# A two-layer attention and expert kernel: the last delay chain of the tail as one block, steps of the attention's set-up and routing moved, the ternary product's ends divided

## The reference, cut to what matters

```
x = x + attention(layernorm(x), ctx)          # 16 heads of 8, causal mask
x = x + experts(layernorm(x))                 # 64 experts, top 8, sigmoid gates normalised by their sum + 1e-8, plus a shared one
x = x + delay_attention(layernorm(x), ctx)    # circular correlation of Q and K by FFT, mean over the channels of a head,
                                              # the 4 best delays, softmax over them, V rolled and summed, then Wo, bo
x = x + ternary(x)                            # layernorm with gamma, beta; weight / (mean|weight| + 1e-5) rounded to -1, 0, 1;
                                              # xn clipped at max|xn| * (128 - 1e-5) / 128; product scaled by mean|weight|
```

## Time and profile before

| | |
|---|---|
| timed runs | 1245.01, 1246.98, 1247.70 us; median 1246.98 |
| the profiled execution's own time | 1246.12 us |
| its span | 1244.3 us (1.8 us lie around it) |
| PE / PE weight load busy | 97% / 80% of the span |
| DVE / ACT / POOL busy | 85% / 74% / 62% |
| mean granted TensorE clock | 0.992 of full |
| attention ends, experts run, tail runs, ternary runs | about 285, to 1090, to 1221, to 1244 us |

### The profile page before, as it was taken

How to read it: one execution, slowest core, us unless ns; L and a number is a source line. 1 busy time by engine, 2 the same in 40 slices (tenths; PEclk the granted TensorE clock), 3 DMA queues, 4 the chain that set the end, 5 groups by cost and what they waited for, 6 DMA issues and landing times. The chain is left out here.

```text
span 1244.3 us, 28539 instructions
## 1 busy us (share of the span) xinstructions
PE 1211.1 (97%) x9899; PEld 993.6 (80%) x9899; DVE 1061.3 (85%) x2053; ACT 922.2 (74%) x1601; POOL 768.6 (62%) x845
## 2 busy tenths in 40 slices
PE   8999999999999999999999999999999999899986
PEld 6878787777888888888888888888888887799975
DVE  6999998997797897987987987978979877699986
ACT  5899998877777777777777677777777776777761
POOL 4667677855576565665665755765656624477773
PEclk8999999999999999999999999999999999999998
DMA  6411111108867767777677687677676775111004
GB/s 147 105 32 34 32 32 32 35 13 196 185 171 180 176 177 173 175 184 175 163 184 182 161 191 183 172 179 178 177 174 174 184 185 142 43 31 31 19 2 135
DMA packets 126174, 159.99 MB, mean 129 GB/s; under 512 B 20840, under 2 KB 59504, under 8 KB 126064
## 3 DMA queue, kind: packets, MB, share of 16 engines
q1 hardware_dynamic: 120976, 156.16, 50.7%
q10 hardware_dynamic: 5088, 2.43, 0.7%
HBM read 152.25 MB, written 6.29 MB: 127 GB/s over the span
## 5 line engine op out<-in xcount | busy, mean ns | idle before, releaser
L1081 POOL TENSOR_TENSOR e_ml<-e_m,e_mh 128x1024 fp32r<-128x1024 f32 x80 | 192.5, 2407 | 145.0 <-ACT e_mh L1234 143.6
L1234 ACT CAST e_mh<-e_m 128x1024 fp32r<-128x1024 f32 x256 | 267.2, 1044 | 6.4 <-DVE e_m L1161 6.4
L1224 ACT ACTIVATE shared<-shared 128x1024 f32<-128x1024 f32 x171 | 172.7, 1010 | 133.0 <-PE shared L1260 131.5
L1166 DVE TENSOR_TENSOR e_ml<-e_m,e_mh 128x1024 fp32r<-128x1024 f32 x176 | 241.7, 1373 | 25.7 <-ACT e_mh L1234 25.7
L1161 DVE TENSOR_TENSOR e_m<-shared,raw 128x1024 f32<-128x1024 f32 x171 | 207.1, 1211 | 61.2 <-ACT shared L1224 61.2
L1270 PE MATMUL e_py<-e_mh,wdl 128*128 128x512 f32 x528 | 209.3, 396 | 0.0
L1269 PE MATMUL e_py<-e_mh,wdh 128*128 128x512 f32 x528 | 208.0, 394 | 0.0
L1273 PE MATMUL e_py<-e_ml,wdh 128*128 128x512 f32 x528 | 167.4, 396 | 0.1
L1258 PE MATMUL shared<-r_xh,wuh 128*128 128x512 f32 x349 | 141.4, 405 | 0.1
L1260 PE MATMUL shared<-r_xl,wuh 128*128 128x512 f32 x349 | 137.9, 395 | 0.0
L1259 PE MATMUL shared<-r_xh,wul 128*128 128x512 f32 x349 | 137.8, 395 | 0.0
(11 more groups left out here) (243 smaller groups left out, 2811.8 us busy)
## 6 DMA issues: line engine op xcount, KB each, us to landing
raw<-gates_scratch SPq DMA_DIRECT2D x512, 256.0 KB, 4.2
x_res<-in_x_dram SPq DMA_DIRECT2D x64, 64.0 KB, 1.8
xcT<-in_ctxT_dram SPq DMA_DIRECT2D x64, 64.0 KB, 1.9
held<-in_ctx_dram SPq DMA_DIRECT2D x32, 128.0 KB, 2.1
raw<-in_L_ffn_W_up_dram SPq DMA_DIRECT2D x4, 512.0 KB, 4.7
raw<-in_L_ffn_W_down_dram SPq DMA_DIRECT2D x4, 512.0 KB, 5.7
gates_scratch<-raw SPq DMA_DIRECT2D x16, 128.0 KB, 2.3
out_dram<-t_res SPq DMA_DIRECT2D x8, 256.0 KB, 2.6
```

Source lines behind the costliest of these rows:

```text
L1081: nc.gpsimd.tensor_tensor(flat(ml[k][:]), flat(m[k][:]), flat(mh[k][:]).bitcast(F32), ALU.subtract).then_inc(m_low[1], 1)
L1166: nc.vector.tensor_tensor(flat(ml[k][:]), flat(m[k][:]), flat(mh[k][:]).bitcast(F32), ALU.subtract).then_inc(m_low[0], 1)
L1224: nc.scalar.activation(flat(pu[k]), flat(pu[k]), ACT.Silu).then_inc(silued, 1)
L1234: nc.scalar.copy(flat(mh[k][:]), flat(m[k][:])).then_inc(m_high, 1)
```

## The change

Attention: the output bias (`p_bias`) is multiplied ahead of step 5 on PE, without the wait for `w_chain` 2, and copied out ahead of step 5's `row_max` on DVE; `weight_mean` takes the place behind it; `p_beta` goes to a free column of the score buffer and into step 5's `scores`. The first chunk's roots stand behind the keys (`expand`) in step 12. The routing weights are made in steps 61 and 62, ahead of the variance operations, and what follows them is one step later.

Tail: group 7's `l_sums` ends in step 34, its chain is correlated in the middle of step 35 behind five extra matmuls, and its eight DVE operations run without a break behind the residual add of step 35 (`CHAIN_STEP`); the turn and transform follow in step 36. From then on POOL's root and offset stand one step later. Extra matmuls that nobody reads (`stay_busy`) are put into the last steps (the entry for `STEPS - 1` falls on a step where `l_pt` no longer runs) and behind them.

Ternary: two and three extra matmuls around the one for the maximum; DVE clips chunk 0 in two parts (128 and 384 columns); the last chunk is added and stored in two halves, one from ACT, one from SP.

```diff
-        p_beta = pob[:, 400:401]
+        p_beta = shared[:, 0, 4 * S:4 * S + 1]
...
-                late = {4: weight_sums, 5: weight_mean, 6: weight_inverse, 7: weight_round, 8: weight_upper, 9: weight_lower}
+                late = {4: weight_sums, 5: output_bias, 6: weight_inverse, 7: weight_round, 8: weight_upper, 9: weight_lower}
...
                     if isinstance(t, int) and t == 5:
-                        dve.wait_ge(o_bias_made, 1)
-                        nc.vector.tensor_copy(braw[:, 2:4, :], p_bias.unsqueeze(1).to_broadcast([3, 2, D])).then_inc(o_bias_out, 1)
+                        weight_mean()
...
                         expand(t - 3, (r - 3) % 2)
+                    if isinstance(t, int) and t == 12:
+                        norms.roots(pool, cst["mhalf"], 0, idle["pool"])
...
+                    if isinstance(t, int) and t == looped + 13:
+                        routing.weigh_all(pool, nc.gpsimd, "pool", 0)
+                    if isinstance(t, int) and t == looped + 14:
+                        routing.weigh_top(pool, nc.gpsimd, "pool", 0)
                     if live(t, 0, n_tiles):
...
-                    if isinstance(t, int) and t == 12:
-                        norms.roots(pool, cst["mhalf"], 0, idle["pool"])
-                    if isinstance(t, int) and t == looped + 13:
-                        routing.weights(pool, nc.gpsimd, "pool", 0)
-                    if isinstance(t, int) and t == looped + 15:
+                    if isinstance(t, int) and t == looped + 16:
                         routing.gates_of(pool, nc.gpsimd, "pool", 0)
...
@@ in scores @@
+                    if isinstance(t, int) and t == 2:
+                        pe.wait_ge(w_chain, 1)
+                        nc.tensor.matmul(p_beta, cst["ones"][:], wabs[:], start=True, stop=True).then_inc(w_summed, 1)
...
                         pe.wait_ge(w_out, 1)
+                        nc.tensor.matmul(p_bias, bv1col[:].to_broadcast([P, 3]), cst["w1T"][:, 3, :], start=True, stop=False)
+                        nc.tensor.matmul(p_bias, cst["ones"][0:1, 0:3], bo1row[:], start=False, stop=True).then_inc(o_bias_made, 1)
...
+    LAST_GROUP = N // 4 - 1
+    CHAIN_STEP = N + 3
...
@@ POOL, tail @@
-                    if on(s, 11):
-                        n = s - 11
+                    lag = 11 if s < CHAIN_STEP else 12
+                    if on(s, lag) and s != CHAIN_STEP:
+                        n = s - lag
...
@@ DVE, tail, behind the add of step 35 @@
+                    if s == CHAIN_STEP:
+                        top_of(LAST_GROUP)
+                        shift(LAST_GROUP)
+                        mark(LAST_GROUP)
+                        choose(LAST_GROUP)
+                        keep(LAST_GROUP)
+                        add_up(LAST_GROUP)
+                        invert_sum(LAST_GROUP)
+                        scale(LAST_GROUP)
...
+                    if on(s, 4) and s != CHAIN_STEP:
+                        sum_up(s - 4)
+                    if s == CHAIN_STEP - 1:
+                        sum_up(N - 1)
...
@@ PE, tail @@
+                def stay_busy(count):
+                    for _ in range(count):
+                        nc.tensor.matmul(pf[0][:, 0, 0, :], cst["ident"][:], cst["ident"][:], start=True, stop=True)
...
+                    if s == CHAIN_STEP:
+                        stay_busy(5)
+                        correlate(LAST_GROUP)
...
+                    if s == CHAIN_STEP + 1:
+                        turn_weights(LAST_GROUP)
...
+                    if s == CHAIN_STEP + 1:
+                        transform_weights(LAST_GROUP)
...
+                        stay_busy({STEPS - 3: 2, STEPS - 2: 4, STEPS - 1: 6}.get(s, 0))
...
+                stay_busy(4)
...
@@ DVE, ternary @@
-                clip(0)
+                for some in (slice(0, P), slice(P, 512)):
+                    nc.vector.tensor_scalar(columns(0)[:, some], columns(0)[:, some], bound[:, 0:1], bound[:, 1:2], ALU.min, ALU.max).then_inc(clipped_dve, 1)
                 clip(1)
...
+                for half in range(2):
+                    dve.wait_ge(multiplied, CHUNKS + half)
+                    add_rows(CHUNKS - 1, 2 * half, 2 * half + 2, (py[3][:, 0:2, :], pg_half)[half])
...
@@ PE, ternary @@
+                stay_busy(2)
                 pe.wait_ge(chain, 2)
                 nc.tensor.matmul(pg[:, 0:P], cst["ones"][:], diag[:], start=True, stop=True).then_inc(across, 1)
+                stay_busy(3)
...
-                sp.wait_ge(stored, 16 * CHUNKS)
+                store_half(sp, 1)
+                sp.wait_ge(stored, 16 * (CHUNKS + 1))
```

More of the change, by code:

```diff
@@ L1710, in _ @@
                     if g is not None:
[L1711 to L1715 removed]
+                        transform_weights(g)
                     if on(s, 2):
@@ L1725, in _ @@
                     k = group(s, 7)
-                    if k is not None:
-                        pe.wait_ge(summed, 4 * (k + 1))
-                        at_least(pe, c_out, k)
-                        at_least(pe, chosen, k)
-                        if k == 0:
-                            pe.wait_ge(preset, 1)
-                        for i in range(2):
-                            ins = nc.tensor.matmul(ext[:, :, 0:S], sums[:, k % 2, i, :], cst["idft_corr"][:, i * P:i * P + P],
-                                                   start=(i == 0), stop=(i == 1))
-                        ins.then_inc(correlated, 1)
+                    if k is not None and k != LAST_GROUP:
+                        correlate(k)
+                stay_busy(4)
 def ternary(nc, cst, x_res, xnT, amax, out, sem):
@@ L1780, in clip, with add_rows @@
                     nc.vector.tensor_scalar(columns(c), columns(c), bound[:, 0:1], bound[:, 1:2], ALU.min, ALU.max).then_inc(clipped_dve, 1)
-                clip(0)
+                for some in (slice(0, P), slice(P, 512)):
+                    nc.vector.tensor_scalar(columns(0)[:, some], columns(0)[:, some], bound[:, 0:1], bound[:, 1:2],
+                                            ALU.min, ALU.max).then_inc(clipped_dve, 1)
                 clip(1)
-                for c in range(CHUNKS):
+                def add_rows(c, first, last, product):
+                    nc.vector.scalar_tensor_tensor(res[:, c, first:last].rearrange("p j d -> p (j d)"),
+                                                   product.rearrange("p j d -> p (j d)"), cst["beta"][:],
+                                                   x_res[:, 4 * c + first:4 * c + last, :].rearrange("p j d -> p (j d)"),
+                                                   ALU.mult, ALU.add).then_inc(summed, 1)
+                for c in range(CHUNKS - 1):
                     if c + 3 in BY_DVE:
@@ L1800, in _, with stay_busy @@
             def _(pe):
+                def stay_busy(count):
+                    for _ in range(count):
+                        nc.tensor.matmul(py[3][:, 0, :], cst["ident"][:], cst["ident"][:], start=True, stop=True)
+                stay_busy(2)
                 pe.wait_ge(chain, 2)
                 nc.tensor.matmul(pg[:, 0:P], cst["ones"][:], diag[:], start=True, stop=True).then_inc(across, 1)
+                stay_busy(3)
                 for c in range(CHUNKS):
                     by_dve = sum(b <= c for b in BY_DVE)
-                    if c in BY_DVE:
-                        pe.wait_ge(clipped_dve, by_dve)
-                    else:
+                    if c in BY_DVE and c > 0:
+                        pe.wait_ge(clipped_dve, by_dve + 1)
+                    if c not in BY_DVE:
                         pe.wait_ge(clipped_pool, c + 1 - by_dve)
```

102 lines of the change are left out of this document (68 added, 34 removed).

## The result

The changed kernel's median is 1237.97 us (five runs, 1236.96 to 1241.75) against 1246.90 for the kernel before beside it; the ratio is 0.9935, interval 0.9918 to 0.9953. The forecast was 1238.7, from 1235.8 to 1243. The profiled execution of after took 1237.64 us with a span of 1235.8: 8.48 us less than that of before, where the sum had 7.45.

The account below looks back on a forecast made before the run. PE, busy 97% of the span at 0.992 of full clock, was taken as the bound. Attention 3.3, chain 2.3, extra matmuls 0.55 and ternary 1.3 gave 7.45 us off 1246.12: 1238.7 us, range 1235.8 to 1243.

Parts of the forecast that it names:

- Output bias: Attention step 6: PE's wait of 1.08 us for DVE's bias copy goes; 1.0 us saved, between 0.7 and 1.1.
- Clock of step 6: Attention: without the wait the clock stays up and step 6 falls from 5.43 to 4.11 us; 1.3 us, low end 0.
- The rival that it falls all the same: Step 6's clock still drops, through narrow or moved set-up matmuls: 1.3 us less, 1240.0 us, chance 0.12.
- My sign of being wrong: Whole kernel: the low clock only moves to another window, or the looped steps, 4.12 us each, change at all.
- Roots: Attention steps 12 and 13: keys come sooner, the 0.66 us wait goes, up to 0.6 comes back; 0.3 us saved.
- Routing weights: Attention steps 61 and 62: the scores' wait of 0.81 us for POOL's keys goes; 0.7 us, bounds 0.3 and 0.8.
- Chain: Tail's last delay chain: ends 3.8 us sooner, but PE's walk limits the gain to 2.3 us, bounds 1.1 and 2.8.
- Extra matmuls: End of tail: holding the clock at 2.4 GHz shortens the last turn and the maximum; 0.55 us, low end -0.3.
- ternary: Ternary stage: first sum 0.7 us sooner, transfers starved 0.6 us less; 1.3 us, bounds 0.2 and 2.4.
- The rival with the largest chance: End of tail: the clock falls despite extra matmuls, losing 0.55 and 1.1 of ternary's 1.3; 1240.3 us, chance 0.23.
- The price that I had put on exclusive ports: Ternary: DVE clips wait for all of POOL's, first sum stays put; forecast 0.7 us longer, 1239.4 us, chance 0.05.
- The slower rival: Attention's loop of 32 steps: each DVE norm falls under POOL's keys, 10.6 us lost; 1249.3 us, chance 0.04.

Follow-up runs that it names:

- the second experiment: The kernel before with five extra matmuls filling PE's wait for the bias copy in step 6, the wait itself kept; median 1246.5 us, ratio 0.9997.
- The tenth experiment: The changed kernel with POOL's old order in attention: roots last in step 12, both routing weights in step 61; median 1240.61 us, ratio 0.9950.
- the seventh experiment: The changed kernel with POOL's root and offset in the tail at lag 11 throughout, as before; median 1239.33 us, ratio 0.9930.
- the third experiment: The changed kernel without the extra matmuls in and behind the tail's last steps and around the maximum, the chain's five kept; median 1242.08 us, ratio 0.9957.
- the eighth experiment: The changed kernel with chunk 0 clipped whole by DVE in one operation of 512 columns; median 1239.02 us, ratio 0.9929.
- experiment 4: The changed kernel with the tail's old schedule and delay chain, the extra matmuls at the end kept; median 1242.01 us, ratio 0.9961.
- the ninth experiment: The changed kernel with chunk 0 clipped whole by DVE and all other chunks clipped by POOL; median 1239.63 us, ratio 0.9936.
- The first: The changed kernel's attention alone, with tail and ternary stage as in the kernel before; median 1244.0 us, ratio 0.9976.
- the twelfth experiment: The changed kernel with nine extra matmuls in PE's waits in attention's early steps; median 1238.36 us, ratio 0.9920.

## Why the prediction was right, point by point

**Output bias, 1.0 forecast, 1.5 found.** The wait went, as said. From the end of PE's wait for `w1T` to step 6's first `weigh` it was 21.19 - 16.36 = 4.83 us and is 19.67 - 16.29 = 3.38. 1.08 of the difference of 1.45 is the wait. I had let 0.25 us of PE's work lose its cover. It did (the wait for `w1T` is 0.78 us now, 0.26 before), but 0.37 us more than the wait went all the same: the bias's matmuls now push the next turn past a wait of 0.20 us for ACT that stood in step 5 before; the rest I can't place. That both kernels had `w1T` within 0.07 us of the same time is luck, as the starts of the experiments show.

**Clock of step 6, 1.3 forecast, 1.4 found.** The mechanism was right as far as one profile against one can show it, and the second experiment shows it apart from the wait. The rival that it falls all the same is out for this step. My sign of being wrong, a low clock that only moves to another window, didn't show in after, but the second experiment's profile has one at 1081 us.

**Roots, 0.3 forecast, 0.6 found.** The step of my working that failed is the price taken from DVE's norm beside POOL's keys, 0.97 us. Beside the root the norm took 0.34, in all eleven profiles that have the two side by side, so nothing came back: step 13 is 0.73 us shorter (3.95 instead of 4.68), and 0.1 of that is lost elsewhere between steps 7 and 14. An operation that is long on POOL needn't be one that stops DVE.

**Routing weights, 0.7 forecast, 0.6 found.** The wait gave 0.88 between the first `weigh` of steps 61 and 63, and the later sums took some 0.26 back up to the experts. The tenth experiment puts the roots and the weights together at 1.4.

**Chain, 2.3 forecast, 2.8 found**, the upper bound. PE's walk through the steps was right in form and 0.4 to 0.5 us late in each: with the attention's 4.16 us added back, the four `l_py` that I had put at 1200.8, 1203.0, 1205.2 and 1207.3 came at 1200.4, 1202.5, 1204.7 and 1206.9. The scale ended 3.6 us sooner, near the 3.8 said. What I had not read is that the clock was at 1.2 GHz from 1197.4 to 1200.8 in the kernel before; the prediction names two places with a low clock, step 6 and the end of the tail, and this is a third, missed. That this spell is the half microsecond wasn't tested by itself. I also gave the move of POOL's root no value; by the seventh experiment it is 0.6 us.

**Extra matmuls, 0.55 forecast, 0.57 found; ternary, 1.3 forecast, 1.0 found.** The rival with the largest chance, a clock that falls at the end all the same, is out: the third experiment gives it back with all its marks (0.66, 0.80, 0.50) when the matmuls go. In the first chunk my middle value, 0.7, came close to the 0.56 found, but for a reason that doesn't hold. I had argued from the overlap of two rows that the port isn't exclusive. In fact DVE's clips are not done until 0.2 to 0.3 us behind POOL's, in before (1224.31 behind 1224.03) as in after. The overlap that I read is best taken as a row that begins while its instruction is held. By the Trainium skill (SBUF — State Buffer, Who interferes with whom) whoever issues first blocks the other for the whole instruction: the trace of after agrees for both of POOL's first clips, and doesn't for its root, which DVE's norm of 0.34 us ran beside. The step that failed is thus the overlap of the two clips. It cost little by luck: what the clock gave (0.7 us of the first chunk, by the third experiment) made up for what the port took, and the eighth experiment gets back 0.35 us at the first sum. The price that I had put on exclusive ports, a first sum that stays where it was, was wrong too, since that sum waits for PE's products of chunk 0 and not for DVE's next clip. The halves of the last chunk weren't tested by themselves.

**The slower rival** is out: steps 14 to 61 took 196.30 us before and 196.31 after. Its price was also short of its name: the 1249.3 us that it gives lies below 1249.5, where I had slower begin.

**The range.** Its ends are not the sums of the terms. With the lower bounds as they stand, attention 1.0, tail 0.8 and ternary 0.2, the high end is 1244.1 us and not 1243.5; the terms named for the low end come to 1.46 us, so 1237.2 and not 1236.

In all each term came within 0.5 us, and the differences (bias +0.5, clock +0.1, roots +0.3, weights -0.1, chain +0.5, ternary -0.3) are the 1.0 us by which the sum was short. The match is in part luck, and looser than it looks: the start moved step 6 by up to 3.5 us from one execution to another, the first delay chain can take 1.6, and neither is of the change.

## What to carry to other kernels

A wait of TensorE of about a microsecond or more in the midst of dense work can cost twice, once as the wait and once as the half speed behind it: 3.4 us of it cost 1.4 to 1.6 us here, behind the wait of 1.08 us and, in five of fourteen profiles, behind one of 2.15. Extra matmuls that nobody reads, put into the wait, kept the clock up in step 6 though the wait stayed. Compare two kernels by the length of a stage within one execution before comparing totals, because a spell of low clock elsewhere is as large as most single edits. Taking the other work out from between the halves of a chain on VectorE was the small part of the gain here (0.46 us of 2.8); its place in the steps, POOL's order around it and the clock were the rest.

## What the runs showed of the hardware that was not expected

**The low clock is partly chance.** Three places had it in every profile: the unfilled wait of 1.08 us in step 6 (one profile, before), the old last chain (four), and the end of the tail without extra matmuls (four). The second is chance too, by the run with a mean clock of 1.000 in experiment 4. Two places had it in some: the start, in eleven of the twelve profiles without matmuls in its waits and for some 3 to 13.6 us, and the first delay chain with its wait of 2.15 us, in five of fourteen.

**PEclk can show 1.00 while matmuls run at half speed.** In the ninth experiment the pair of matmuls at 14.74 took 1.22 us with 1.00 beside it, in the fourth the same pair at 13.81 took 1.22 with 0.50. The first, seventh and eighth have such pairs under 1.00 as well, so a mean granted clock can leave out a spell of the start. The duration of a known matmul is the surer sign near the start.

**The shared port stops some operations and not others.** DVE's clip of 384 columns ends 0.22 us behind POOL's clip and its next one 0.28 us; in the twelfth experiment it is POOL's clip that is held up, 1.13 us instead of 0.82; yet DVE's norm (0.34 us) ran inside a POOL operation of 1.04 us that raises 128x4 numbers to a power, at full speed. Which operations of POOL hold the port was not measured further.
